# Summing four weighted corners on TensorE instead of VectorE, in every stage of three sampled passes

## The reference

```
py = dy + row + ky ;  px = dx + column + kx            # 9 taps, learned offsets
g00, g01, g10, g11 = the four neighbours of (py, px), all 64 channels (0 outside)
val = g00*(1-wy)*(1-wx) + g01*(1-wy)*wx + g10*wy*(1-wx) + g11*wy*wx
val = val * mask
out[o, position] = sum over channel c and tap k of val[c, k, position] * weight[o, c, k] + bias
```

## Time and profile before

| | |
|---|---|
| median of 3 runs | 9129.32 us |
| profiled execution: its own time, span | 9125.77 us, 9124.0 us |
| first pass (preparation alone) ends, sampling begins | 1384 us |
| first sampled pass: chunks, norm, taps, convolution, two loops, cosines, offsets end at | 1826, 1908, 2687, 2875, 2983 and 3078, 3190, 3403 us |
| final stage | 7483 to 9104 us |
| busy share of the span: PE, DVE, ACT, POOL | 54%, 71%, 24%, 61% |
| mean granted clock of TensorE | 0.747 |

### The profile page before, as it was taken

The page is one execution under the profiler, slowest core; times in us unless marked ns, Lnnn a source line. Parts: engine busy times, 40 slices in busy tenths (PEclk is TensorE's granted clock), DMA queues, the critical chain, the costliest instruction groups (busy, mean ns, idle before and its releaser), DMA issues. The chain is left out here.

```text
span 9124.0 us, 81228 instructions
## 1 busy us (share of the span) xinstructions
PE 4956.5 (54%) x23346; PEld 2991.4 (33%) x23346; DVE 6478.7 (71%) x7381; ACT 2144.6 (24%) x3720; POOL 5591.5 (61%) x5206
## 2 busy tenths in 40 slices
PE   4555665656656555666656556566656552222222
PEld 3333223434433234434433234344433231111111
DVE  5699557789985767789985767789985754444444
ACT  1344232232322312222322312223212310000000
POOL 0000007767777757767777657767777667777776
PEclk7877787778878777778878777788877775555555
DMA  2000033332233543332233543332233533333333
GB/s 75 21 0 0 21 115 98 106 97 78 80 102 107 158 133 102 106 95 79 78 105 107 161 132 105 103 95 80 78 107 107 164 115 113 112 113 113 112 112 104
DMA packets 443180, 887.26 MB, mean 97 GB/s; under 512 B 119073, under 2 KB 268919, under 8 KB 439925
## 3 DMA queue, kind: packets, MB, share of 16 engines
q0 software_dynamic: 248832, 679.81, 25.4%
q1 hardware_dynamic: 190708, 129.65, 4.9%
q10 hardware_dynamic: 3456, 75.50, 2.0%
HBM read 763.04 MB, written 121.53 MB: 97 GB/s over the span
## 5 line engine op out<-in xcount | busy, mean ns | idle before, releaser
L655 POOL DMA_INDIRECT gathered_corners<-gather_table,metas x5184 | 5583.2, 1077 | 3510.9 <-issue 2855.1
L1409 PE MATMUL ps<-ident,sampled 128*128 128x128 f32 (+1 forms) x2160 | 482.8, 377 | 2393.8 <-DVE sampled L734 1271.7
L1165 ACT COPY sampled_by_channel<-ps 128x512 f32<-128x512 f32 x576 | 336.5, 584 | 3933.2 <-PE ps L1409 3131.4
L1481 PE MATMUL ps<-region,woff 128*128 (+1 forms) x3456 | 1192.2, 502 | 23.6 <-ACT region L1150 23.6
L1409 PEld LDWEIGHTS ps<-ident,sampled 128*128 128x128 f32 (+1 forms) x2160 | 320.4, 181 | 2612.3 <-issue 2085.7
L717 DVE TENSOR_TENSOR gathered_corners<-gathered_corners,ps 128x2304 f32<-128x2304 f32 x288 | 735.5, 2554 | 453.8 <-DMA gathered_corners<-gather_table,metas 445.1
L1481 PEld LDWEIGHTS ps<-region,woff 128*128 128x128 f32 x3456 | 670.3, 197 | 494.4 <-issue 50.6
L1406 PE MATMUL ps<-ident,weighted_corners 128*128 128x128 f32 (+1 forms) x2880 | 534.2, 366 | 526.2 <-DVE weighted_corners L715 526.2
L1393 PE MATMUL ps<-sampled_by_channel,w 128*64 128x256 f32 x2880 | 688.0, 462 | 0.0
L1406 PEld LDWEIGHTS ps<-ident,weighted_corners 128*128 128x128 f32 (+1 forms) x2880 | 475.6, 187 | 617.3 <-issue 453.5
L907 DVE TENSOR_TENSOR work<-work 128x768 f32<-128x768 f32 x720 | 664.1, 951 | 5.0
(11 more groups left out here) (229 smaller groups left out, 7941.8 us busy)
## 6 DMA issues: line engine op xcount, KB each, us to landing
gathered_corners<-gather_table,metas POOLq DMA_INDIRECT x5184
x_after_layer<-region ACTq DMA_DIRECT2D x8, 4608.0 KB, 13.2
gather_table<-tabst SPq DMA_DIRECT2D x192, 192.0 KB
region<-in_x_dram ACTq DMA_DIRECT2D x12, 1536.0 KB, 11.2
region<-x_after_layer ACTq DMA_DIRECT2D x4, 4608.0 KB, 14.8
res<-x_after_layer SPq DMA_DIRECT2D x144, 128.0 KB
out_dram<-ob SPq DMA_DIRECT2D x144, 128.0 KB
indices_and_weights<-region SPq DMA_DIRECT2D x16, 810.0 KB
```

What stands on the lines that cost most here:

```text
L655: pool.indirect_dma_start(out=G[:, s % NG, k, :], out_offset=None, in_=table, in_offset=bass.IndirectOffsetOnAxis(ap=idx[:, s * KK + k:s * ...
L1165: nc.scalar.copy(VT[:, i, 0:4, 128 * t2:128 * t2 + 128], ps[:, 5, :].rearrange("p (k n) -> p k n", k=4))
L1409: mm = pe.transpose(out_m, V[:, s % 2, 128 * m:min(128 * m + 128, KK * C)], ident[:, :])
L1481: mm = pe.matmul(ps[:, b, 0:RN], woff[:, e, k, :], conv_rhs(pad2_1, 2, j * 16 + 4 * b, k // 3 - 1, k % 3 - 1), start=k == 0, stop=k == KK - 1)
```

## The change

The argument `False` goes from all calls of `steps_of` in the sampled passes, on DVE and on PE, so that all 144 steps take the True way. The final stage keeps its calls with `False`. `Chain.restart` counts the increment that it makes, since a loop body may now have no other instruction that counts.

```
@@ Chain.restart
             self.after()
             self.engine.sem_inc(self.sem, 1)
+            self.count += 1
@@ VectorE: attention chunk
-                    steps_of(c, slot, (0,), False, first)
+                    steps_of(c, slot, (0,), first=first)
...
-                    steps_of(c, slot, (2,), False)
+                    steps_of(c, slot, (2,))
@@ VectorE: norm, convolution, two loops, cosines
-                    steps_of(G_NORM, G_NORM % 2, NORM_PLACES.get(c, ()), False)
+                    steps_of(G_NORM, G_NORM % 2, NORM_PLACES.get(c, ()))
...
-                        steps_of(j + G_CONV[0], (j + G_CONV[0]) % 2, CONV_PLACES[e], False)
+                        steps_of(j + G_CONV[0], (j + G_CONV[0]) % 2, CONV_PLACES[e])
...
@@ VectorE: offsets
-                        steps_of(h + G_OFFSETS, (h + G_OFFSETS) % 2, (s,), False)
+                        steps_of(h + G_OFFSETS, (h + G_OFFSETS) % 2, (s,))
@@ TensorE: the same places
-                    steps_of(c, (0,), False)
+                    steps_of(c, (0,))
...
-                        steps_of(h + G_OFFSETS, (s,), False)
+                        steps_of(h + G_OFFSETS, (s,))
```

More of the change, by code:

```diff
@@ L795, in chunk @@
                         ch.named(ch.after().tensor_tensor(ek4[:, i], kps, wide(kmax[:, i]), ALU.subtract), k_sub, c * 2 + (i + 1))
-                    steps_of(c, slot, (1,), False, first)
+                    steps_of(c, slot, (1,), first=first)
                     for i in range(2):
@@ L825, in chunk @@
                             ch.named(ins, at_cp, c + 1)
-                    steps_of(c, slot, (3,), False)
+                    steps_of(c, slot, (3,))
                     if not last:
@@ L854, in _ @@
                 v.nop().then_inc(borders, 1)
-                steps_of(G_NORM, G_NORM % 2, (2, 3), False)
+                steps_of(G_NORM, G_NORM % 2, (2, 3))
                 v.wait_ge(x1_stored, 16)
@@ L1033, in _ @@
                     for e in range(12):
-                        steps_of(j + G_CONV[1], (j + G_CONV[1]) % 2, SUM_PLACES[e], False)
+                        steps_of(j + G_CONV[1], (j + G_CONV[1]) % 2, SUM_PLACES[e])
                     ch.restart()
@@ L1038, in _ @@
                         t = j * 12 + e
-                        steps_of(j + (G_CONV[1] + 2), (j + G_CONV[1]) % 2, SUM_PLACES[e], False)
+                        steps_of(j + (G_CONV[1] + 2), (j + G_CONV[1]) % 2, SUM_PLACES[e])
                         v.wait_ge(c2_mm, t + 1)
@@ L1061, in _ @@
                         ins.then_inc(prods, 1)
-                        steps_of(j + G_COSINES, (j + G_COSINES) % 2, COSINE_PLACES[e], False)
+                        steps_of(j + G_COSINES, (j + G_COSINES) % 2, COSINE_PLACES[e])
                     ch.restart()
@@ L1070, in _ @@
                 v.nop().then_inc(cst_zeroed, 1)
-                steps_of(G_OFFSETS, G_OFFSETS % 2, (0, 1), False)
+                steps_of(G_OFFSETS, G_OFFSETS % 2, (0, 1))
                 v.wait_ge(dots_loaded, 96)
@@ L1443, in _ @@
                         mm.then_inc(q_mm, 1)
-                    steps_of(c, (1,), False)
+                    steps_of(c, (1,))
                     for i in range(2):
@@ L1456, in _ @@
                         mm.then_inc(m_mm, 1)
-                    steps_of(c, (2,), False)
+                    steps_of(c, (2,))
                     pe.wait_ge(m_cp, c * 2 + 2)
@@ L1470, in _ @@
                     mm.then_inc(y_mm, 1)
-                    steps_of(c, (3,), False)
+                    steps_of(c, (3,))
                 group_mean(1, oct_avg[:, :])
-                steps_of(G_NORM, (0, 1), False)
+                steps_of(G_NORM, (0, 1))
                 group_mean(2, pair_avg[:, :])
@@ L1499, in _ @@
                     offset_bank(0, 0, b)
-                    steps_of(G_NORM, ((), (2,), (3,), ())[b], False)
+                    steps_of(G_NORM, ((), (2,), (3,), ())[b])
                 for e in range(2):
@@ L1522, in _ @@
                     conv_quadrants(q)
-                    steps_of(q // 3 + G_CONV[0], CONV_PLACES[q % 3], False)
+                    steps_of(q // 3 + G_CONV[0], CONV_PLACES[q % 3])
                 group_mean(3, pair_avg[:, :])
@@ L1535, in _ @@
                         mm.then_inc(c2_sum, 1)
-                        steps_of(j + G_CONV[1], SUM_PLACES[e], False)
+                        steps_of(j + G_CONV[1], SUM_PLACES[e])
                 pe.wait_ge(c2_copied, RT + 4)
@@ L1543, in _ @@
                                   start=True, stop=True).then_inc(c2_mm, 1)
-                        steps_of(j + (G_CONV[1] + 2), SUM_PLACES[e], False)
+                        steps_of(j + (G_CONV[1] + 2), SUM_PLACES[e])
                 group_mean(4, pair_avg[:, :])
@@ L1562, in _ @@
                         mm.then_inc(n_tr, 1)
-                        steps_of(j + G_COSINES, COSINE_PLACES[tile], False)
+                        steps_of(j + G_COSINES, COSINE_PLACES[tile])
                 pe.wait_ge(cos_cp, RT + 2)
```

## The result

The changed kernel takes 9038.42 us (median of 4 runs, 9033.54 to 9040.03) beside 9129.71 us before: a ratio of 0.9899, 95% interval 0.9882 to 0.9916. It is faster by 91 us; 9005 was forecast. The profiled execution has a span of 9037.2 us against 9124.0.

A forecast was written before the change was run, and what follows sets the result against it. POOL's gathers were taken to pace most stages, DVE and PE the rest. Terms of -30.5, -17.3, +3.4 and +3 gave -41.4 us a pass, x 3 = -124, from 9125.77 to 9001.6, adjusted to 9005; range 8975 to 9040.

The forecast's parts named there:

- A, the holds: Chunks, convolution, first loop, cosines: removing adds with two SBUF inputs stops them holding gathers, -30.5 us a pass.
- the end of a group: Five places, in convolution, first loop, cosines and second loop: shorter DVE path less a longer turn, -1.2 us each.
- the rival by which the holds stay: Gathers are held by something else DVE does, so only 11 us a pass is gained: 9096 us, chance 0.08.
- B, VectorE's shorter path: Where gathers or group ends wait for DVE, its path is 2.26 us a step shorter: -17.3 us a pass.
- the projection behind it starts warmer: At group ends the turn grows about 1.7 us, but the following projection runs faster, 3.73 against 6.14: +1.06 net.
- C, turns ahead of the last bank: Two longer PE turns ahead of the last offset bank, 1.69 us each, delay it without cover: +3.4 us.
- D, the offsets stage: Longer PE turns and the single product buffer lengthen the offsets stage: +3 us a pass, bounds 0 to +17.
- PE's 17 us: In the offsets stage, where PE is always busy, 10 longer turns add 10 x 1.69 = 17 us.
- the cover: The pass's last 56 us of gathers and DVE work hide 14 of 17 us of added PE work in offsets.
- Its slower rival: Offsets: single buffer makes product, turn and gathers alternate, PE gets holes, clock falls; 9339 us at 0.50; chance 0.08.
- Late PE by slow transposes: Rival: added transposes run at 1.20 GHz, costing offsets +15 and second loop some +9 a pass: 9078 us, chance 0.14.
- Outside the passes: Outside the sampled passes nothing changes; the restart count adds one clear per loop, nothing that shows: 0 us.

The follow-up runs named there:

- experiments 5 and 6: Changed kernel plus two unused VectorE adds after each product in chunks and convolution: both inputs in SBUF 9108.51 us, one in PSUM 9015.84 us.
- experiment 4: Changed kernel with two product buffers used by turns instead of one: 8995.62 us, ratio 0.9861 to the kernel before.
- experiment 5: Changed kernel plus two unused VectorE adds, both inputs in SBUF, after each product in chunks and convolution: 9108.51 us, ratio 0.9983.

## Why the prediction was right, and where a size was off

**A, the holds (-30.5 forecast): right, a little small.** Chunks -18.7 (16.2 was taken); inner convolution, first loop and cosines as worked out: the 14 steps from 90 to 103 take 7.6, 6.9 and 5.7 us less in the three passes (8.0 for 16), the first loop 4.5 (3.6, and 1.2 for the end of a group), the cosines behind their first gap 2.8 as a mean (2.7). The mechanism stands by experiments 5 and 6, and the rival by which the holds stay is gone.

**B, VectorE's shorter path (-17.3): half right.** Where the adds alone were ahead of gathers it came: norm -7.1 by its gathers, with the last offset bank beginning 5.3 us earlier on PE (6.8 was taken), start of the convolution -2.0 (gap 10.6 to 8.6 us). The step that failed is that "the projection behind it starts warmer", "+1.06 net". The last turn of the second loop before, and in the changed kernel (PE, then the DVE instruction that waits):

```profile
3065.60 1.32 PE L1409 MATMUL ps<-ident,sampled 128*128 128x128 f32 x5 [5.45 <-DVE sampled L722]
3066.85 4.54 PE L1393 MATMUL ps<-sampled_by_channel,w 128*64 128x256 f32 x20
3071.32 2.20 PE L1542 MATMUL ps<-work,w 96*128 x6
...
3072.47 0.62 DVE L1042 SCALAR_TENSOR_TENSOR region<-ps,chan,region 128x384 f32 x1 [5.27 <-PE ps L1542]
```

```profile
3036.63 4.52 PE L1407 MATMUL ps<-ident,weighted_corners 128*128 128x128 f32 x20 [3.67 <-DVE weighted_corners L716]
3041.08 4.45 PE L1394 MATMUL ps<-sampled_by_channel,w 128*64 128x256 f32 x20
3045.46 2.20 PE L1543 MATMUL ps<-work,w 96*128 x6
...
3046.61 0.62 DVE L1043 SCALAR_TENSOR_TENSOR region<-ps,chan,region 128x384 f32 x1 [8.44 <-PE ps L1543]
```

The turn grew from 1.32 to 4.52 us, since it starts with the clock down: 0.50 over the whole turn in this row (the columns of the earlier trace rows).

```profile
3036.70:3041.00 4.30, 4.30 (x20) 3.88 (x20) 1.29 (x3) 0.00 (x0) 3.39 (x4) 0.50 0.40 115
```

The projection went from 4.54 to 4.45 only; its first 2 us have a clock of 0.61 in both kernels. Net +3.1, where +1.06 was taken, against 2.26 us of adds: DVE waits 8.44 instead of 5.27 us. So no group's end in this loop was worth -1.2. And the second loop and the start of the cosines are paced by the preparation: gathers that got ahead in the loop (0.4 to 1.0 us a step, 0 was taken) gave it back in the gap ahead of the third step of the cosines, 18.41 us in the row below and 14.77 before:

```profile
3068.27 1.33 POOL L656 DMA_INDIRECT gathered_corners<-gather_table,metas  x1 [18.41 <-DVE weighted_corners L716]
```

These two stages gave 4.3 in place of 8.6 us.

**C, turns ahead of the last bank (+3.4): right.** In the changed kernel the bank on PE, with the two turns in it, and then the DVE instruction that waits for it:

```profile
1859.21 14.76 PE L1482 MATMUL ps<-region,woff 128*128 128x384 f32 x36 [5.92 <-ACT region L1151]
1873.81 2.35 PE L1407 MATMUL ps<-ident,weighted_corners 128*128 128x128 f32 x20
1875.99 6.00 PE L1482 MATMUL ps<-region,woff 128*128 128x384 f32 x18
1881.83 2.34 PE L1407 MATMUL ps<-ident,weighted_corners 128*128 128x128 f32 x20
```

```profile
1894.02 0.96 DVE L889 TENSOR_TENSOR work<-ps,neg_y 128x768 f32<-128x768 f32 x1 [14.05 <-PE ps L1482]
```

The turns grew from 0.71 to 2.35 and 2.34 us, 3.3 together, as taken. In this first pass the first 36 matmuls took 1.4 us more too; before, the bank began so:

```profile
1877.74 13.36 PE L1481 MATMUL ps<-region,woff 128*128 128x384 f32 x36 [5.92 <-ACT region L1150]
```

From the bank's first matmul to L889 (L888 in the earlier trace rows) it is 34.8 us, 30.1 before. As means of the three passes it is 34.4 and 30.9: +3.5, and the 1.4 us are of the first pass alone (14.62 and 14.33 us before in the other two, 14.18 and 13.94 after). Norm and taps together gained 0.9 instead of 3.4 since the bank began only 5.3 us earlier (B), and 1.0 us more went behind it.

**D, the offsets stage (+3): direction right, size too small.** +5.8 was measured, within the bounds 0 to +17. PE's 17 us came as 15.9; the step that was mis-sized is the cover, taken as 14 us of tail and measured as 10.2 (table of experiment 4). The single buffer keeps it small: one product waits 34.67 us for the turn of the step before, POOL's gathers wait with it, and with two buffers the tail is 8.8 us shorter still. The prediction had named that wait and took it with PE's work as one term. Its slower rival built on it did not come: it needed gaps in PE's work, and there are none from 3198.60 us to the preparation's last matmul, at a clock of 0.98 (the changed kernel, columns of the earlier trace rows):

```profile
3198.60:3331.50 132.90, 132.90 (x866) 79.62 (x866) 66.87 (x99) 22.74 (x66) 81.67 (x85) 0.98 0.38 117
```

**Late PE by slow transposes: no.** Turns in PE's busy stretch of the offsets run at the granted clock of 1.00, and ahead of the bank 20 transposes took 2.35 us. Where the clock is down at a turn's start, the turn takes some 4.5 us, which is what B missed.

**Outside the passes (0): 7.4 us against the change in the profiled executions.** The first pass ended at 1384.3 us before and at 1389.8 after; in the other kernels, with the same code there, it ended between 1384.8 and 1388.1. So this is scatter of an execution; the medians differ by 91 us, the spans by 87.

The forecast's own range, 8975 to 9040, just holds the 9038, and that is partly luck: the chunks gave 2.5 us a pass more than was taken, 7.5 in all, without which the time would be above it. The terms that were too good, B and D, both count a wait on TensorE.

## What to carry to other kernels

Work that is moved from a busy engine to an idle one is paid where the idle engine is waited for: price it at the clock that it finds there, not at its best. A single buffer is enough as long as its consumer follows at once; where the consumer's turn stands behind other work in program order, a second buffer can be worth as much as less work (12.0 and 15.5 us of a stage here), even with the consumer's engine busy all the time. If VectorE works beside GpSimd's gathers, try one operand in PSUM: here it kept them at 0.95 us.

## What the runs showed of the hardware that was not expected

Two adds of the same sizes and durations on VectorE (1.36 and 0.76 us from SBUF, 1.35 and 0.75 with one input in PSUM) differ by 92.7 us over the 3 x 52 steps that have them, 0.59 us a step. "SBUF — State Buffer", section "Who interferes with whom", of the Trainium skill says that a VectorE instruction with two SBUF inputs contends with GpSimd's reads. That is borne out by the 92.7 us. It infers that a tensor_tensor does not stall descriptor generation; for the gather as a whole that does not hold here: one took 1.62 us and one 1.25 us (experiment 5) beside a tensor_tensor. Which part of a gather waits, no run shows.

Turns of transposes ran at either level of the clock: 20 took 2.35 and 2.34 us in the last offset bank, where the clock was 1.00, and 4.52 us at 0.50 in the second loop. The Trainium skill, "TensorE: Matmul & The Clock Gate", section "Part 4: PE-mode transpose", says that the full clock does not engage for transposes; these turns at 1.00 do not bear that out where other matmuls stand around them, and the only row of transposes alone ahead of a rise to 1.00 is that in the earlier trace rows.
